# A graph layer with experts: the weights' split beside the mix, the first norm in the prologue, the bias fold by columns

## The reference, cut to what matters

```python
xn = _layernorm(x)
# graph part: degree embeddings, two sigmoid terms, edge sums by source node
in_deg, out_deg = segment_sum(1, dst), segment_sum(1, src)            # capped at 511
gnn = xn + z_in[in_deg] + z_out[out_deg] + sigmoid(cent @ W_cent + b) \
         + sigmoid(vor @ W_vor + b) + segment_sum(edge_attr @ W_sum + b_sum, src)
# mix: 8 heads of 64, keys and values normalised in each head, dots over all nodes
q, k, v = split(xn @ w_qkv, 3);  k, v = inst_norm(k), inst_norm(v)
mix = (q @ (k^T v) / n) @ w_out + b_out
x = x + gnn + mix
# experts: layer norm, router, the best 2 of 8 experts (256 -> 1024 -> 256), weighted sum
h = gelu((norm(x) * ln_g[e] + ln_b[e]) @ W1[e] + b1[e]);  y = h @ W2[e] + b2[e]
out = x + sum over the top 2 of weight * y
```

## Time and profile before

| | us |
|---|---|
| median of 3 runs | 2552.91 |
| lowest, highest | 2547.14, 2553.13 |
| span of the profiled execution | 1904.7 |

### The profile page before, as it was taken

One profiled execution on the slowest core, in us unless ns is written; L12 is line 12 of the kernel. 1 busy time (PEld: TensorE's weight loads), 2 busy tenths in 40 slices (PEclk: granted clock), 3 DMA queues, 4 the chain that ended last, 5 costly groups with the idle time before them and its releaser, 6 DMA issues.

```text
span 1904.7 us, 37327 instructions
## 1 busy us (share of the span) xinstructions
PE 1604.6 (84%) x11699; PEld 1268.2 (67%) x11699; DVE 1397.2 (73%) x3345; ACT 742.3 (39%) x1618; POOL 1359.2 (71%) x1290
## 2 busy tenths in 40 slices
PE   5556554798999989999977778937999999999996
PEld 1121222455666669999866777836998999889896
DVE  6789776866878768886578777996666666666664
ACT  0001111454444435545500776734444444444432
POOL 5777787777777777777777788804666666666654
PEclk9767765799999999999999999967999999999998
DMA  6378778734545448999999997764999999999984
GB/s 179 107 231 265 227 239 236 209 106 137 147 135 142 139 117 214 233 231 230 242 285 294 256 297 182 165 191 166 269 268 271 283 273 267 267 285 269 276 249 121
DMA packets 380659, 414.33 MB, mean 218 GB/s; under 512 B 50006, under 2 KB 295438, under 8 KB 380462
## 3 DMA queue, kind: packets, MB, share of 16 engines
q1 hardware_dynamic: 220120, 218.17, 37.5%
q10 hardware_dynamic: 102390, 101.63, 20.6%
q0 software_dynamic: 57952, 92.15, 18.8%
HBM read 316.11 MB, written 95.67 MB: 216 GB/s over the span
## 4 chain that ended last, share of the span: by engine, by line
PE 57%; DVE 16%; POOL 8%; issue 7%; ACTq 4%; DMA 3%; ACT 3%; DVEq 1%; SPq 1%; POOLq 0%
PE bank L926 15%; PE bank L940 14%; POOL sorted_rows L1883 7%; PE bank L691 7%; PE bank L806 7%; PE bank L673 3%; DVE big L1182 3%; ACTq L2043 2%; PE bank L784 2%; PE bank L840 2%; PE bank L849 1%; DVE big L1195 1%; PE bank L912 1%; DMA w_parts<-big 1%; PE bank L618 1%
## 5 line engine op out<-in xcount | busy, mean ns | idle before, releaser
L1883 POOL DMA_INDIRECT sorted_rows<-edge_rows,sorted_pos x780 | 813.3, 1043 | 239.2 <-issue 214.2
L1836 ACT ACTIVATE mixw<-bank,edge_rows 128x256 f32<-128x256 f32 (+1 forms) x456 | 241.7, 550 | 322.8 <-PE bank L926 231.9
L926 PE MATMUL bank<-edge_rows,big 128*128 128x256 f16 (+1 forms) x2736 | 287.7, 265 | 0.5 <-issue 0.5
L940 PE MATMUL bank<-big 128*128 128x256 f16 x2520 | 284.4, 273 | 1.0 <-issue 1.0
L926 PEld LDWEIGHTS bank<-edge_rows,big 128*128 128x128 f16 x2736 | 249.4, 97 | 31.0 <-issue 1.0
L940 PEld LDWEIGHTS bank<-big 128*128 128x128 f16 x2520 | 244.1, 98 | 28.6 <-issue 1.3
L1968 POOL DMA_INDIRECT result<-mixw,edge_rows x105 | 168.9, 1609 | 129.1 <-DVE mixw L1614 68.7
L1182 DVE TENSOR_TENSOR big<-big,bank 128x128 f32 x592 | 169.6, 286 | 81.7 <-DVE big L1182 10.6
L691 PE MATMUL bank<-big 128*128 128x128 f32 x1440 | 179.6, 279 | 25.6 <-DVE big L1195 19.0
L691 PEld LDWEIGHTS bank<-big 128*128 128x128 f32 x1440 | 169.7, 193 | 34.0 <-DVE big L1195 23.7
L806 PE MATMUL bank<-mixw,xnT 128*128 128x512 f32 x392 | 183.0, 610 | 5.4 <-ACT mixw L1738 5.4
(11 more groups left out here) (368 smaller groups left out, 2798.0 us busy)
## 6 DMA issues: line engine op xcount, KB each, us to landing
big<-w_parts SPq DMA_DIRECT2D x114, 1024.0 KB, 6.7
edge_rows<-edge_attr SPq DMA_DIRECT2D x78, 640.0 KB
big<-sorted_rows ACTq DMA_DIRECT2D x296, 129.0 KB
big<-sorted_rows SPq DMA_DIRECT2D x128, 129.0 KB
big<-L_ffn_W ACTq DMA_DIRECT2D x128, 128.0 KB
w_parts<-big ACTq DMA_DIRECT2D x64, 256.0 KB, 4.1
mixw<-sorted_rows ACTq DMA_DIRECT2D x104, 129.0 KB
sorted_rows<-edge_rows,sorted_pos POOLq DMA_INDIRECT x780
```

The costliest lines, as they stand in the source:

```text
L926: ins = e.matmul(ps_h[h % 4][:, w], W1r[:, r, a, k, h * P:(h + 1) * P], xT[:, r, b, k, w], start=(k == 0 and s == 0), stop=(k == KC - 1 an ...
L940: ins = e.matmul(ps_o[s][:, 0:DIM], hT[:, r, a, h, s * P:(s + 1) * P], W2r[:, r, b, h, :], start=(h == 0 and i == 0), stop=(h == HC - 1 an ...
L1836: e.activation(h32[:, h, w], ps_h[h % 4][:, w], ACT.Gelu, bias=m_r[:, n, h:h + 1], scale=m_r[:, n, HC:HC + 1]).then_inc(gelu_done, 1)
L1883: e.indirect_dma_start(sorted_rows, bass.IndirectOffsetOnAxis(ap=row_pos[:, c:c + 1], axis=0), rows, None, bounds_check=last_row, oob_is_e ...
```

## The change

The split gets a schedule of its own, `WEIGHT_AT`, over ticks 14 to 126. The side stream keeps norm, mix, fold and rest: the norm in ticks 0 to 11, the mix from tick 14 to 148, the fold to 158. So split and mix now share ticks, the split's steps ahead of the mix's in each tick. PSUM banks are dealt out anew: the split's small results leave bank 5 (the mix's dots) and banks 6 and 7 (keys and values) for banks 1 and 2. These are the visits' banks, so the visits start at tick 128, behind the split. All of x is loaded by ACT at the start; 28 tiles' statistics stand in ticks 0 to 11, those of 21 tiles between the dependent steps of the visit table. Four memsets move ahead of the counts. The bias fold takes the weights as the stationary side and one column of `ln_b` as the moving one, which gives its result in the layout that is wanted; the copies and the transposes fall away.

```diff
-W_TICK0, W_TICKS = 2, (2 * EXPERTS - 1) * WEVERY + 15
+W_TICK0, W_TICKS = 2, (2 * EXPERTS - 1) * WEVERY + 14
 W_META = W_TICK0 + W_TICKS
-NORM_END = 1 + 4 * XCH
-MIX0, MIX_EVERY = NORM_END + 51, 2
+NORM_STEPS, NORM_FILL = 16, 28
+NORM_END = 1 + NORM_STEPS
+MIX0, MIX_EVERY = NORM_END + 1, 2
...
-SIDE_AT = ((START, 0), (92, W_TICK0 + W_TICKS), (190, FOLD0), (TICKS - 12, SIDE_STEPS))
+WEIGHT_AT = ((START, 0), (126, W_META + 1))
+SIDE_AT = ((0, 0), (START - 3, NORM_END), (START, MIX0), (148, FOLD0), (158, REST0), (TICKS - 12, SIDE_STEPS))
...
-DEGREE_AT = ((148, 0), (166, SHARED + 4), (262, DEGREE_STEPS))
-VISIT_TICKS = ((104, 0), (176, EARLY), (196, EARLY), (TICKS, VISIT_AT[2] // VB))
+DEGREE_AT = ((148, 0), (158, SHARED + 4), (272, DEGREE_STEPS))
+VISIT_TICKS = ((128, 0), (176, EARLY), (186, EARLY), (TICKS, VISIT_AT[2] // VB))
...
+    ps_b1 = banks[1][:, 0:EXPERTS * HC]
+    ps_peak, ps_top = banks[2][0:1, 0:P], banks[2][:, P:P + 1]
...
@@ tensor_visit, b == 0
             e.wait_ge(tabled, TABLE_ALL)
+            e.wait_ge(b1_dve, 5)
+            e.wait_ge(w_scaled, scale_ops(2 * EXPERTS - 1) + 1)
@@ tensor_fold_b1
-        for c in range(2):
-            ins = e.matmul(ps_kv[c][0:EXPERTS, :], offset[:, k, ex * EXPERTS:(ex + 1) * EXPERTS],
-                           raw[r][:, k * HID + c * INNER:k * HID + (c + 1) * INNER],
-                           start=(ex == 0 and k == 0), stop=(ex == EXPERTS - 1 and k == KC - 1))
+        for h in range(half * HC // 2, (half + 1) * HC // 2):
+            c = ex * HC + h
+            for k in range(KC):
+                ins = e.matmul(ps_b1[:, c:c + 1], raw[r][:, k * HID + h * P:k * HID + (h + 1) * P], ln_t[:, 1, ex, k:k + 1],
+                               start=(k == 0), stop=(k == KC - 1))
@@ tensor_weights
-            if at_stage(w, 7, WEVERY, 2 * EXPERTS) == EXPERTS - 1:
-                e.wait_ge(b1_kept, 1)
-                for h in range(HC):
-                    ins = e.transpose(ps_kv[0][:, h * EXPERTS:(h + 1) * EXPERTS], b1_fold[:, h * P:(h + 1) * P],
-                                      ident[0:EXPERTS, 0:EXPERTS])
-                ins.then_inc(b1_turned, 1)
@@ tensor_mix
-            if t == 0:
-                e.wait_ge(w_scaled, scale_ops(2 * EXPERTS))
@@ tensor_program, and alike on DVE and ACT
+            for u in weight_steps(tick):
+                tensor_weights(e, u)
             for u in side_steps(tick):
-                tensor_weights(e, u)
                 tensor_mix(e, u)
...
+    def vector_zeros(e):
         e.memset(XL[:, ECOLS - LOADS * LOAD, 0:EDIM], 0.0).then_inc(edge_const, 1)
+        e.memset(state[:, TILES - 1, :], 0.0).then_inc(edge_const, 1)
+        e.memset(bias_m, 0.0).then_inc(edge_const, 1)
+        e.memset(bias_s, 0.0).then_inc(edge_const, 1)
+        e.wait_ge(edge_const, EDGE_ZEROS - 1)
+        e.memset(bias_s[BROW:BROW + 1, :, :], 1.0).then_inc(edge_const, 1)
...
@@ vector_visits, then()
             ins.then_inc(tabled, 1)
+            vector_norm(e, 2 * NORM_FILL + steps[0] - TABLE_BASE[1] - 1)
             e.wait_ge(tabled, steps[0])
...
+    def vector_norm(e, i):
+
+        t, second = divmod(i, 2)
+        if t >= TILES:
+            return
+        if second:
+            e.wait_ge(norm_dve, 2 * t + 1)
+            e.bn_aggr(mv[:, t, :], stats[:, t % 2, :]).then_inc(norm_dve, 1)
+        else:
+            if t % XPER == 0:
+                e.wait_ge(x_load[t // XPER], 64)
+            e.bn_stats(stats[:, t % 2, :], state[:, t, :]).then_inc(norm_dve, 1)
...
@@ vector_program
+        vector_zeros(e)
         vector_index(e)
@@ scalar_weights
-        if at_stage(w, 6, WEVERY, 2 * EXPERTS) == EXPERTS - 1:
-            e.wait_ge(w_folded, EXPERTS)
-            for c in range(2):
-                ins = e.copy(b1_fold[:, c * INNER:(c + 1) * INNER], ps_kv[c][0:EXPERTS, :])
-            ins.then_inc(b1_kept, 1)
@@ scalar_load_mix
         if u == 0:
-            load_x(e, 0)
-        if 1 <= u < NORM_END:
-            i, s = divmod(u - 1, 4)
-            if s == 0 and i + 1 < XCH:
-                load_x(e, i + 1)
-            if s == 3:
-                load_small(e, i)
+            for i in range(XCH):
+                load_x(e, i)
+            for s in range(5):
+                load_small(e, s)
```

92 lines of the change are left out of this document (42 added, 50 removed).

## The result

The changed kernel takes 2528.57 us where the kernel before takes 2553.02 beside it: a ratio of 0.9894, with a 95% interval from 0.9857 to 0.9932. That is faster by 1.1%, and outside my range (2542 to 2563). One of the changed kernel's four executions took 3199.33 us, at a granted clock of 0.548 where the others had 0.84 to 0.86; it is in the median but not in the ratio, and no run tells what it was.

What follows compares the result with a forecast made beforehand. POOL's chain of scatters and gathers was taken to bound the first 1246 us. Loop 0, first batch and clock 0, POOL's loss -1, norm 0, x +1, fold 0 left the span at 1904.7 us, hence 2553 us, range 2542 to 2563.

Steps and rivals of the forecast that it cites:

- the 648.2 us around the span: Time between the profiled span of 1904.7 us and the runs' median of 2552.91, taken to stay unchanged.
- POOL never waits: Scatters and gathers, about 20 to 1240 us: POOL runs at its own pace and bounds the first 1246 us.
- the zero for the overlap: Tick loop: 55 to 85 us gained becomes a wait of ACT before part three, so 0 on the span.
- Split and mix side by side: Tick loop, 115 to 984 us: ends at 900 to 930, but part three's first load stays at 984; 0.
- earlier first batch: First batch of part three: the queue is empty at 984, so its add comes sooner; -2 us, between -3 and 0.
- low clock: First batches of part three: PE at the lower clock level, at most two batches, 0 to +4 us.
- POOL's loss: Scatters in the loop: 51 us lost to DVE instructions with two SBUF inputs stays; 5 instead of 9 comparisons, -1 us.
- x loaded at the start: Start: ACT's loads of x get in the way of the src load for chunk 0; +1 us, 0 to +3.
- Norm: 0: Prologue: statistics moved to ticks 0 to 11 and the visit table, covered by the ranks' lead; 0 us.
- fold: 0: Bias fold by 256 one-column products, covered by idle PE and the loop's 55 us; 0, without cover up to 46.
- The loop ends after POOL: Slower rival, ticks 14 to 148: PE at clock 0.65, loop ends at 1026; +42 us, 2595; chance 0.13.
- the overlap pays in full: Faster rival, tick loop: 2553 less 55 to 85 us, near 2480, if part three starts without chunk 69; chance 0.01.

Runs made afterwards that it cites:

- e1: Kernel before, unchanged, profiled again in a timed run with standstills: 1.0013 of before, 2548.96 us.
- e11: Changed kernel, unchanged, run without standstills: 0.9964 of the kernel before, 1905.33 us.
- e3: Changed kernel with the four schedule tables of the kernel before, split then mix, with standstills: 1.0157 of the kernel before, 2588.41 us.
- e2: Changed kernel, unchanged, profiled a second time, with standstills: 0.9823 of the kernel before, 2504.08 us.
- e10: Kernel before with only the early loads of x and small weights and the norm's statistics in the prologue, without standstills: 0.9997 of before.
- e16: Kernel before with only the early loads of x and small weights and the norm's statistics in the prologue, with standstills: 1.0077 of before.
- e4: Kernel before with only the new bias fold by one-column products, without standstills: 1.0036 of before.
- e5: Changed kernel with half of the fold's one-column products left out, without standstills: 0.9963 of the kernel before.
- e14: Kernel before with plain DMAs in place of the scatters by position, sort left out, with standstills: 0.7973 of before, 2030.26 us.

## Why the prediction was wrong, point by point

**The step that failed** stands in one sentence: "the 648.2 us around the span, which no row shows, I leave". A third more time than the profiled execution holds isn't a constant beside it: e1 has the whole of it inside its span (2543.4 us for a time of 2545.16), 403 us as standstills and the rest as shorter waits and slower matmuls under the scatters and in the work left behind them. The difference said that the profile and the times weren't of one condition, and that every slack I read was unproven for the runs to be predicted. I should have made the case "in the timed runs something stalls under the first half" a rival with a price. The overlap lets other work go on when one stream is held, so its sign would have been faster.

**POOL never waits.** Right for the condition of the profile (e11: 239.2 us idle, as before), wrong for the timed runs of both kernels (124.9 us of waits for ranks in 15 pieces in e1, 163.7 in 18 after). This is what carried the zero for the overlap, which with the rest of the tables is worth 84 us there (e3 beside e2).

**Split and mix side by side.** I had the loop end at 900 to 930, a gain of 55 to 85 us turned into a wait before part three, and the load at 984. In e11 the loop ends at 915, the gap is 74.5, the load is at 983.95. The two small terms behind it, earlier first batch and low clock, which I set at 0 together, cancel as well: the first add that waits for PE is at 995.16 instead of 995.37, since PE, at a granted clock of 0.60 from 989 to 997, needs some 4 us for the first 16 products instead of 2.05. In the timed condition there is no such gap; the whole change gains 34 to 41 us there.

**POOL's loss.** -1 us for 5 instead of 9 comparisons with row numbers from SBUF. The count is right, the form below stands 5 times in e11; the scatters' mean, 1044 instead of 1043 ns, leaves the sum at nothing. That two-input instructions stretch scatters, which I took from one row, holds over the whole trace of before: the 90 scatters beside which DVE has nothing but TENSOR_TENSORs with both inputs in SBUF take 1097 ns in the mean and up to 1812, the 128 beside TENSOR_TENSORs with an input from PSUM alone take 975 and never over 997, and the 60 beside no DVE instruction 975.

```profile
L1201 DVE TENSOR_TENSOR big<-iota,big x5: 1225/1225/1227, 512.6 to 538.8; 128x1024 f32<-128x1024 f32 x5
```

**x loaded at the start.** +1 us: the first scatter is at 20.1 instead of 19.0 in e11, and the row of e10 gives 0.9997. With standstills the same edit costs 0.8%, 20 us, all in the scatter stage (e16; early loads and early norm together). Why so much more there, no run tells.

**Norm: 0** and **fold: 0.** Without standstills the norm is inside e10's 0.9997. The fold alone costs 0.4% (e4), where I had named up to 46 us without cover and 0 with it; within the changed kernel, under the gap, half of it less changes nothing (e5 against e11), as argued.

**The 7 us left.** Without standstills the changed kernel is 0.36% faster, 3 to 10 us, and I had said none; e5 has the same on another chip (0.9963). Its profiled execution, 1910.03, was one of its longer ones, and it shows no step that is earlier: scatters end at 1086 instead of 1084, the last node addition starts at 1249.9 instead of 1246.1. So this stays open. The forecast of no change describes this condition well, but it was made for times of the other; that it lies within 1.1% of the result is luck, since the 639 us between the two conditions stood outside its sum.

**The rivals.** None of them was the case. "The loop ends after POOL" had the right place and the wrong sign: under the standstills the loop does end after POOL, in both kernels. The one on the other side of the sum, that the overlap pays in full, had 0.01 on the ground that part three can't start before chunk 69; true, and beside the point once POOL itself waits.

**Why the scatters hold the others.** The runs name the cause, not the way. By the Trainium skill, "DMA: Bandwidth & Descriptors", section "SWDGE vs HWDGE vs iDMA", descriptors of DMAs from GpSimd, direct and indirect, are made by software and written to rings in SBUF. The page makes no difference between them. e14 and e1 do: both kinds run on the queue `q0 software_dynamic` in their pages, and only the indexed ones hold others up. The Trainium skill, "NOTIFIC — the notification-queue block", section "Overflow: three behaviours, one of which stalls the engine", describes one way in which recording itself can stop a producer. That could hold updates too, but no run here tested it. For it speaks that 71 of the 162 PE updates between 120 and 600 us and 246 of the 489 of DVE have no event in the trace of e1, and next to none is missing without standstills (0 of 405 and 2 of 834 in that of before). But this may as well be a consequence: runs of both conditions were recorded, and no run was made unrecorded.

## What to carry to other kernels

Compare the span of the profiled execution with the timed runs before anything else. Where they differ by more than a per cent, explain that first, since a slack read from one condition proves nothing for the other. Where DMAs with lists of positions are issued back to back over a long stage, look whether the semaphore updates of the other engines come late and in bursts, and try short instructions between them on the issuing engine: here 0.05 us more between two gave 5%, and 0.2 us more gave 16% together with the overlap. Without standstills the 0.05 us cost 1.7%.

## What the runs showed of the hardware that I had not expected

- Two conditions for one program: 1909 to 1912 us on two chips, 2528 to 2550 on five, and before steady within each session (for example 1905 to 1923 and 2531 to 2556). What sets them apart no run shows, nor whether a chip can change from one to the other.
- In the second, updates of PE's semaphores come late under indirect scatters at a pitch of 1.28 us: 7 us after the last instruction that can have made them, by the events seen in e1 and in the profile after, and 20 and 11 us where a missing event counts with the next. Under plain DMAs on the same queue, with as many packets, they don't (0.01 us). In the expert stage of e1 POOL issues 303 instructions in 600 us, not 369 in 485, and PE is busy 569 of the 600.
- The price of a pause is far below its worth there: eight one-column memsets, 0.21 us a scatter, took PE's mean lag between 120 and 600 us, counted with missing events, from about 20 us in e1 to about 3.
- With PE idle under the standstills its granted clock is low (0.56 and 0.65 in 115 to 600 us of e1 and after, against 0.91 in e11), so part of the lost time is longer matmuls: PE is busy 1671.5 us in e1 and 1604.6 in the earlier trace rows, for the same instructions.
- A scatter's issue takes 975 ns beside DVE instructions that read PSUM, and 1097 in the mean beside TENSOR_TENSORs with both inputs in SBUF (trace of before).
